# q, k and v projections contracted as 128 plus 64, biases moved, in an attention and expert kernel

## What is computed

```python
h = tok(x, tables, ln_scale, ln_bias)
xt = layernorm(h)
qkv = xt @ qkv_w.T + qkv_b
q, k, v = split(qkv)                      # 12 heads of 16 a batch entry, 4 entries of 512 tokens
attn = softmax(einsum(q, k) * D ** -0.5)
out = einsum(attn, v) @ proj_w.T + proj_b
t = out / norm(out)                       # per head
sim = einsum(t, t) * 10, negative ones masked, softmax
out2 = einsum(sim, v) @ proj_w.T + proj_b
h = h + out2
h = h + experts(layernorm(h))
```

## Time and profile before

| | |
|---|---|
| median of three runs | 669.4 us |
| the profiled execution | 666.99 us |
| its span, first to last instruction | 665.2 us |
| TensorE matmuls busy | 546.1 us (82%) |
| VectorE busy | 459.2 us (69%) |
| ScalarE busy | 333.1 us (50%) |
| GpSimd busy | 230.9 us (35%) |
| TensorE clock granted, mean | 0.932 of full |

### The profile page before, as it was taken

One profiled execution on the slowest core, in us unless ns is written; L12 is line 12 of the kernel. 1 busy time (PEld: TensorE's weight loads), 2 busy tenths in 40 slices (PEclk: granted clock), 3 DMA queues, 4 the chain that ended last, 5 costly groups with the idle time before them and its releaser, 6 DMA issues.

```text
span 665.2 us, 11966 instructions
## 1 busy us (share of the span) xinstructions
PE 546.1 (82%) x3482; PEld 322.5 (48%) x3483; DVE 459.2 (69%) x1008; ACT 333.1 (50%) x762; POOL 230.9 (35%) x278
## 2 busy tenths in 40 slices
PE   0256989998999999989996888433899999999991
PEld 0131423342335223433243333221799999999991
DVE  3669999889888999888678989459534334334330
ACT  0030557656778788768965877100233333333330
POOL 6841331224423151102211310001256665665641
PEclk9985989989999999989997999855799999999997
DMA  4155034013905263210431569730123323333321
GB/s 116 38 77 65 6 78 63 5 41 65 127 6 96 48 96 50 45 61 17 80 49 55 94 134 263 218 121 31 57 46 54 51 45 55 47 49 55 48 34 17
DMA packets 40561, 45.00 MB, mean 68 GB/s; under 512 B 10403, under 2 KB 34853, under 8 KB 40518
## 3 DMA queue, kind: packets, MB, share of 16 engines
q0 software_dynamic: 12864, 19.97, 18.0%
q1 hardware_dynamic: 27654, 24.52, 17.0%
HBM read 17.88 MB, written 7.60 MB: 38 GB/s over the span
## 4 chain that ended last, share of the span: by engine, by line
PE 59%; DVE 25%; issue 6%; DMA 5%; ACT 3%; POOL 0%; POOLq 0%; DVEq 0%; SPq 0%; ACTq 0%
PE psum L1087 11%; PE psum L939 10%; PE psum L1071 7%; PE psum L1000 5%; DVE MX L713 5%; PE psum L1076 4%; PE psum L976 4%; DVE arena L727 4%; PE psum L992 4%; PE psum L1007 4%; DMA result<-T,slot_dest 3%; PE psum L1029 3%; PE psum L964 2%; DVE X L644 2%; PE psum L1039 1%
## 5 line engine op out<-in xcount | busy, mean ns | idle before, releaser
L554 ACT ACTIVATE arena<-psum 128x512 f32<-128x512 f32 x384 | 207.4, 616 | 51.9 <-PE psum L1000 34.4
L713 DVE TENSOR_REDUCE MX<-psum 128x1 f32<-128x512 f32 x192 | 126.1, 681 | 9.3 <-PE psum L992 9.3
L727 DVE SCALAR_TENSOR_TENSOR arena<-arena 128x1024 f32<-128x1024 f32 x96 | 120.2, 1263 | 9.5 <-ACT arena L554 8.7
L586 ACT ACTIVATE arena<-psum,b_sb 128x128 f32<-128x128 f32 x234 | 64.5, 376 | 108.2 <-PE psum L1076 108.2
L939 PE MATMUL psum<-arena 128*17 128x512 f32 x768 | 104.1, 615 | 5.8 <-DVE arena L727 5.8
L494 POOL DMA_INDIRECT result<-T,slot_dest x39 | 67.8, 1738 | 74.4 <-DMA result<-T,slot_dest 39.2
L1087 PE MATMUL psum<-arena 128*128 x468 | 86.3, 335 | 0.6 <-ACT arena L586 0.6
L355 POOL DMA_DIRECT2D KS<-arena x72 | 36.7, 512 | 121.2 <-ACT arena L535 59.8
L1087 PEld LDWEIGHTS psum<-arena 128*128 128x128 f32 x468 | 75.0, 190 | 5.4 <-issue 0.8
L904 DVE TENSOR_TENSOR T<-psum,arena 128x192 f32<-128x192 f32 x39 | 14.0, 358 | 82.9 <-PE psum L1087 70.9
L992 PE MATMUL psum<-late_stacks,arena 96*128 96x512 bf16 x144 | 58.5, 415 | 14.9 <-DVE MX L713 7.6
(11 more groups left out here) (172 smaller groups left out, 676.1 us busy)
## 6 DMA issues: line engine op xcount, KB each, us to landing
late_stacks<-arena POOLq DMA_DIRECT2D x72, 64.0 KB, 4.2
QS<-arena SPq DMA_DIRECT2D x72, 64.0 KB, 3.8
KS<-arena POOLq DMA_DIRECT2D x72, 64.0 KB, 3.8
arena<-w SPq DMA_DIRECT2D x8, 576.0 KB, 8.1
arena<-arena SPq DMA_DIRECT2D x54, 64.0 KB, 4.1
arena<-w SPq DMA_DIRECT2D x8, 384.0 KB, 7.6
x_rows<-X SPq DMA_DIRECT2D x4, 384.0 KB, 4.5
result<-H SPq DMA_DIRECT2D x4, 384.0 KB, 4.4
```

The costliest lines, as they stand in the source:

```text
L554: act.activation((P1, P2)[ps][:, n % PRING, :], s, ACT.Exp, scale=(QSCALE, SIM_SCALE)[ps]).then_inc(done, 1)
L586: last = act.activation(HT[i][:, hc, :], hid_ps[i][hc], ACT.Gelu, bias=b1_sb[:, bass.ds(e, 1), hc:hc + 1].rearrange("p o h -> p (o h)"))
L713: dve.tensor_reduce(MX[:, g % 2, CT * i + c:CT * i + c + 1], slot(k), AX_X, ALU.max).then_inc(freed[k % RING], 1)
L727: dve.scalar_tensor_tensor(p, p, 1.0, p, ALU.is_ge, ALU.mult).then_inc(masked, 1)
```

## The change

The 192 inputs of a projection are contracted as 128 plus 64. `XT` and `WQKV` hold the first 128 in their first half; the last 64 stand twice, in rows 0 to 63 and 64 to 127 of the second half. The 64-row matmuls of the event pair go to the two row halves of the array. For that both events of a pair come together in the list. ScalarE copies the last 64 rows of X's transpose twice. The q and k bias is added when PSUM is read, by ScalarE and by VectorE. The v bias no longer enters v: at the start TensorE multiplies it with the output projection's weights and bias (the fold), and VectorE writes the result into the bias rows of `PW` and `PWN`.

```diff
-            at(-6 + h if first else a - 15 + j, 0, "q_proj", b, j)
-            at(-5 + h if first else a - 13.5 + j, 0, "k_proj", b, j)
+            at(-6 if first else a - 14.6, 0, "q_proj", b, j)
+            at(-5 if first else a - 12.6, 0, "k_proj", b, j)
...
-            at(-4 + h if first else a - 11 + j, 0, "v_proj", b, j)
+            at(-4 if first else a - 10.6, 0, "v_proj", b, j)
...
-                sp.dma_start(WQKV[0:KW], qkv_wt.rearrange("(k p) m -> p k m", k=KC)).then_inc(wqkv_in, 16)
-                sp.dma_start(WQKV[KW:KW + 1, 0, :], qkv_b.unsqueeze(0)).then_inc(wqkv_in, 16)
+                sp.dma_start(WQKV[:, 0, :], qkv_wt[0:P, :]).then_inc(wqkv_in, 16)
+                for half in range(2):
+                    sp.dma_start(WQKV[half * P // 2:(half + 1) * P // 2, 1, :], qkv_wt[P:C, :]).then_inc(wqkv_in, 16)
+                sp.dma_start(qk_bias[:, :], qk_b).then_inc(wqkv_in, 16)
+                sp.dma_start(v_bias[0:KW, :], v_b).then_inc(v_bias_in, 16)
...
             def _(act):
+                act.wait_ge(wqkv_in, 64)
                 for kind, args in EVENTS:
...
-                        act.activation(XT[0:KW, j, :], s[0:KW], ACT.Copy).then_inc(done, 1)
+                        if j == 0:
+                            act.activation(XT[:, 0, :], s, ACT.Copy).then_inc(done, 1)
+                        else:
+                            act.activation(XT[0:P // 2, 1, :], s[0:P // 2], ACT.Copy)
+                            act.activation(XT[P // 2:P, 1, :], s[0:P // 2], ACT.Copy).then_inc(done, 1)
...
+                            act.activation(PARTS[kind[0].upper() + "H"][:, j, :], s, ACT.Identity,
+                                           bias=bias_of(kind, j)).then_inc(hi_written, 1)
...
-                dve.memset(XT[KW:KW + 1, 0, :], 1.0)
+                dve.memset(v_bias[KW:KW + 1, 1:2], 0.0)
+                dve.memset(v_bias[KW:KW + 1, 0:1], 1.0).then_inc(bias_ones_set, 1)
                 dve.memset(OT[KW:KW + 1, 0, :], 1.0).then_inc(consts_set, 1)
+                dve.wait_ge(biases_folded, 1)
+                dve.tensor_copy(PW[KW:KW + 1, 0, :], psum[0:1, 7, 0:C])
+                dve.tensor_copy(PWN[KW:KW + 1, 0, :], psum[0:1, 7, C:2 * C]).then_inc(biases_kept, 1)
+                dve.wait_ge(wqkv_in, 64)
...
+                            dve.scalar_tensor_tensor(REST[n % RESTS], slot(k), bias_of(kind, args[1]), hi,
+                                                     ALU.add, ALU.subtract).then_inc(freed[k % RING], 1)
...
             def _(pe):
+                pe.wait_ge(pw_in, 64)
+                pe.wait_ge(v_bias_in, 16)
+                pe.wait_ge(bias_ones_set, 1)
+                for n, w in enumerate((PW, PWN)):
+                    for kc in range(KC):
+                        rows = KW + (kc == 0)
+                        last = pe.matmul(psum[0:1, 7, n * C:(n + 1) * C], v_bias[0:rows, kc:kc + 1], w[0:rows, kc, :],
+                                         start=kc == 0, stop=kc == KC - 1)
+                last.then_inc(biases_folded, 1)
                 pe.wait_ge(ident_set, 1)
...
-                        for kc in range(KC):
-                            rows = KW + (kc == 0)
-                            last = pe.matmul(s, WQKV[0:rows, kc, m0:m0 + 2 * GC], XT[0:rows, kc, :], start=kc == 0, stop=kc == KC - 1)
+                        m0 = [C * (kind == "k_proj") + n * GC for n in range(KC)]
+                        pe.matmul(s, WQKV[:, 0, m0[m]:m0[m] + 2 * GC], XT[:, 0, :], start=True, stop=False, skip_group_check=True)
+                        if m == 0:
+                            continue
+                        first = unit(kind, b, 0)
+                        pe.matmul(slot(first), WQKV[0:P // 2, 1, m0[0]:m0[0] + 2 * GC], XT[0:P // 2, 1, :],
+                                  start=False, stop=True, skip_group_check=True).then_inc(filled[first % RING], 1)
+                        last = pe.matmul(s, WQKV[P // 2:P, 1, m0[1]:m0[1] + 2 * GC], XT[P // 2:P, 1, :],
+                                         start=False, stop=True, skip_group_check=True)
```

More of the change, by code:

```diff
@@ L148, in unit, with build @@
     return UNIT[(kind, args)]
-def build(nc, ids, table, ln_scale, ln_bias, qkv_wt, qkv_b, proj_wt, proj_b, proj_wt_n, proj_b_n, gate_wt, w1, b1, w2, b2, out):
+def build(nc, ids, table, ln_scale, ln_bias, qkv_wt, qk_b, v_b, proj_wt, proj_b, proj_wt_n, proj_b_n, gate_wt, w1, b1, w2, b2, out):
     ctx = ExitStack()
@@ L294, in build @@
         y_ps = [psum[:, 6 + i, 0:C] for i in range(2)]
+        v_bias_in, bias_ones_set, biases_folded, biases_kept = (sem(x) for x in ("v_bias_in", "bias_ones_set", "biases_folded", "biases_kept"))
         ids_in, lnw_in, wqkv_in, pw_in, gt_in = (sem(s) for s in ("ids_in", "lnw_in", "wqkv_in", "pw_in", "gt_in"))
@@ L339, in build, with bias_of @@
         LOADS = 16 * len(Q_PARTS)
+        def bias_of(kind, j):
+            n = KC * (kind == "k_proj") + j
+            return qk_bias[:, n:n + 1]
         def lo_part(eng, source, b, j):
@@ L534, in _ @@
                                     act.wait_ge(side[g % len(side)], LOADS * (g // len(side) + 1))
-                        act.activation(PARTS[kind[0].upper() + "H"][:, j, :], s, ACT.Copy).then_inc(hi_written, 1)
+                        if kind == "t_transpose":
+                            act.activation(PARTS["TH"][:, j, :], s, ACT.Copy).then_inc(hi_written, 1)
+                        else:
+                            act.activation(PARTS[kind[0].upper() + "H"][:, j, :], s, ACT.Identity,
+                                           bias=bias_of(kind, j)).then_inc(hi_written, 1)
                     elif kind == "v_proj":
@@ L960, in _ @@
                                 wait_consumed(pe, unit("normalise", g, args[1]))
-                        width, stride = (2 * GC, GC) if kind == "t_transpose" else (KW, KW)
+                        width, stride = {"t_transpose": (2 * GC, GC), "x_transpose": ((P, C - P)[kc], P)}.get(kind, (KW, KW))
                         for c in range(CT):
@@ L967, in _ @@
                         b, m = args
-                        m0 = C * (kind == "k_proj") + m * GC
                         for kc in range(KC):
@@ L981, in _ @@
                         for c in range(2):
-                            for kc in range(KC):
-                                rows = KW + (kc == 0)
-                                last = pe.matmul(slot_tiles(k)[:, c, :], XT[0:rows, kc, (2 * j + c) * P:(2 * j + c + 1) * P],
-                                                 WQKV[0:rows, kc, 2 * C:3 * C], start=kc == 0, stop=kc == KC - 1)
+                            pe.matmul(slot_tiles(k)[:, c, :], XT[:, 0, (2 * j + c) * P:(2 * j + c + 1) * P], WQKV[:, 0, 2 * C:3 * C],
+                                      start=c == 0, stop=False, skip_group_check=True)
+                        if j == 0:
+                            continue
+                        first = unit(kind, b, 0)
+                        for c in range(2):
+                            before_last = pe.matmul(slot_tiles(first)[:, c, :], XT[0:P // 2, 1, c * P:(c + 1) * P], WQKV[0:P // 2, 1, 2 * C:3 * C],
+                                                    start=False, stop=True, skip_group_check=True)
+                            last = pe.matmul(slot_tiles(k)[:, c, :], XT[P // 2:P, 1, (2 + c) * P:(3 + c) * P], WQKV[P // 2:P, 1, 2 * C:3 * C],
+                                             start=False, stop=True, skip_group_check=True)
+                        before_last.then_inc(filled[first % RING], 1)
                     elif kind == "max_unit":
```

16 lines of the change are left out of this document (11 added, 5 removed).

## The result

The changed kernel took 677.38 us (median of 4 runs, 675.6 to 681.33), the kernel before beside it 669.28. The ratio is 1.013, with a 95% interval of 1.0067 to 1.0192: slower, by 8.1 us between the medians and by 8.7 us by the ratio, where 4.5 was forecast. The direction was right, the size was not: the median lies a tenth under the range's upper end of 677.5, the ratio on the forecast's own base of 669.4 us gives 678.1, above it, and the change is nearly twice the forecast one. The profiled execution took 676.36 us, its span is 674.6, against 665.2 in the earlier trace rows.

What follows compares the result with a forecast made beforehand. It took TensorE and VectorE as full in batch 1, TensorE in batches 2 and 3, nothing overlapping at the start. Start 4.8, behind X +1.5 - 1.0, batch 1 +0.8, batches 2 and 3 -1.6: +4.5, 673.9 us, range 669.4 to 677.5.

Steps and rivals of the forecast that it cites:

- the start decides: The forecast itself: the delay at the kernel's start outweighs the rest, +4.5 us in all; chance 0.55.
- The start: Batch 0 up to X: VectorE waits 3.2 us for the fold, growing through GpSimd's clears to +4.8 us.
- +6.5: Upper bound of the delay at X's end, if every operation between two tensors is also blocked by GpSimd's clears.
- Behind X: Batch 0 after X: late table load and second half's copies +1.5 us, TensorE's saving coming back -1.0.
- Batch 1: Batch 1's projections: VectorE is full, so its idling during the q lump is lost, +0.8 us, bounds -1.0 and +2.0.
- Batches 2 and 3: Their projections: TensorE is full, so part of its saving comes through, -1.6 us for both, bounds -3.0 and 0.
- I take 0.8 of the 1.5: In batches 2 and 3, 0.8 us of TensorE's 1.5 saved per batch comes through despite the lumps.
- hidden there: The second XT copy costs ScalarE 0.5 to 0.6 us more a batch, but ScalarE has room for it.
- Bias at the read: Adding biases at ScalarE's and VectorE's PSUM reads costs zero; bounds -0.05 and +0.1 us for each of 16.
- B: Rival: lumps cost nothing, three batches give 1.5 us each, the start costs its lower end; 669.2 us, chance 0.22.
- D: Rival: 64-row tiles take turns or lumps starve VectorE each time, +5.5 to +8.9 us, middle 676.6; chance 0.16.
- C: Rival: fold is over before the first gathered rows, so VectorE waits for nothing new; 665.4 us, chance 0.07.

Runs made afterwards that it cites:

- Experiments 2: Changed kernel with VectorE's wait for the fold and the fold's two copies moved behind X of batch 0; ratio to before 1.008.
- 12: Changed kernel with VectorE's fold wait and ScalarE's bias wait moved later, and one XT copy instead of two for the second transpose (columns 64 to 191); ratio 1.0126.
- 13: Kernel before, with GpSimd's stack clears made to wait until X of batch 0 is written; 664.0 us, ratio 0.9924.
- experiment 3: Changed kernel with VectorE's fold wait moved behind X and ScalarE's bias wait moved to its first read of q; ratio to before 1.0048.
- 14: Changed kernel with both start waits moved, one XT copy for the second transpose, and GpSimd's clears held until X is written; ratio to before 1.0004.
- experiment 9: Changed kernel with both start waits moved, old order, no pairs, each second matmul zero-padded to 128 rows; ratio to before 1.0122.
- experiment 1: Kernel before, with only the two events of each projection pair put together at the changed due times; ratio 1.0029.
- 11: Kernel before, unchanged, run again for a second profile; ratio 0.999.
- 10: Kernel before with the lumps alone, plus the first half's filled signal held back to three quarters of the lump; ratio 1.0024.
- experiment 7: Changed kernel with both start waits moved, q and k unpaired in the old order, v still paired; ratio to before 1.0273.
- 5: Changed kernel with both start waits moved, old order, each event doing its own 64-row matmul unpaired; ratio to before 1.0235.
- 6: Changed kernel with both start waits moved, lumps kept, each event doing its own 64-row matmul unpaired; ratio to before 1.0367.

## Why the prediction was wrong

The forecast was +4.5; the two profiles differ by 9.4, the runs by 8.7 by their ratio. The forecast's view that the start decides holds for half of this. The other half is what it had wrong: batches 2 and 3 are 4.4 us off it, batch 1 is 1.1.

- **The start, +4.8 forecast, +4.0 measured.** The fold was ready 0.6 us earlier than reckoned (VectorE 2.6 late, not 3.2). That the delay grows through the clears was right, but not where. The forecast had two of the norm's small operations held up and X waiting for the last clear alone. Measured, the last of those small ones ran at 23.33, ahead of the first clear (23.68), and the growth came within X, which met three clears instead of two (6.05 us instead of 4.52). Experiments 2, 12 and 13 show both parts, the wait and the clears. That X's price hangs on when GpSimd clears was seen; that the same place could give 3 us was not.
- **Behind X, +1.5 - 1.0 forecast, +0.6 measured** (4.65 - 4.02). Right in both parts: the projections start 4.4 us behind X where they started 2.8, and 1.0 comes back. Of the late table load's 1.28 us only 0.5 reaches the first maximum (experiment 3).
- **Batch 1, +0.8 forecast, +1.9 measured.** Under-sized, near its bound of +2.0. One copy does not change it (23.45 in 14 against 23.47), so it is not the copy; and experiment 9, with the copy, the biases and the fold but without lumps and pairs, loses only 0.2 (21.75), so some 1.7 goes with the lumps and pairs. How they share it isn't settled: the kernel with lumps alone lost 0.7 (22.25), at another clock.
- **Batches 2 and 3, -1.6 forecast, +2.8 measured in the first profiles (1.1 + 1.7), +3.2 at equal clock (1.4 + 1.8): the step that failed.** It took the saving as coming through, less some waiting. It had three parts, and each was off the same way. "I take 0.8 of the 1.5": the lumps cost 0.8 and 1.35 by themselves (experiment 1 against 11). The second XT copy, "hidden there", costs 0.6 and 0.7 (12 against the change). And of the 1.5 a batch that TensorE saves, 0 and 0.3 arrive: 25.77 in 12 against 25.77 in 1, and 29.24 against 29.57. The saving itself was sized right, 2.87 us for a lump against the forecast 2.9. But it lies ahead of a point where TensorE waits for VectorE, and the pair makes the chain of reads behind the lump longer by as much; this cause is read from the traces (see 10), where the sizes are measured by edits. The longer reads of the biases, which 12 has and 1 has not, hide at most some 0.1 us of a gain in each: experiment 9 has them too and loses 0.7 and 0.8, of which the copy is 0.6 and 0.7.
- **Bias at the read, 0 forecast.** A record takes 0.75 us against 0.69 on VectorE and 0.68 against 0.60 on ScalarE: small, within the bounds given.
- **The rivals.** B (lumps cost nothing) is out. D came nearest in size, but its mechanism, tiles that take turns, did not happen. It was the other half of D, "or the lumps starve VectorE each time", that held. C needed the weights by 8.1 us; they came at 10.66.

The Trainium skill (SBUF — State Buffer, Who interferes with whom) kept +6.5 out of the range, and the trace agrees: the small operations with two inputs ran on beside the clears, and X, operations with one, took 6.05 us and in another profile 7.65. The Trainium skill (TensorEngine Tiling (Array Packing), Key Properties) warned of the drain at a switch; its size here is 0.29 us, as read before the change, 3.5 us for the twelve unpaired switches of two batches.

## What to carry to other kernels

A saving on a full engine counts only up to its next wait: ask which engine the first instruction behind the saved ones waits for, and whether that engine's own chain got shorter. Making two results ready together puts their reads in series; that may eat what the pairing saves. And an operation of 0.6 us on an engine with time to spare is not free where another engine waits for the slot that it holds.

## What the runs showed of the hardware

- Lone 64-row tiles between full ones went with a TensorE that stayed at half speed: full speed came first at 75.5 (experiment 7), 79.5 (5) and 112.8 us (6), and in all other profiles, those with pairs too, between 30.6 and 41.9 us. Replacing the tiles by zero-padded ones (9) undid it. The two kernels differ in nothing else that TensorE does, so the edit shows the tiles as the cause; how the chip comes to it isn't shown.
- VectorE's four operations of one input took 1.35, 4.5, 6.05, 6.99 and 7.65 us (experiment 13, before, changed, 5, 12), as they met none, two, three, four (the first already under way) and four of GpSimd's clears of 1.85 us.
